# Theta behind the prediction, GpSimd's small operations ahead of the entry's low part, the last two sums in one reduction, and preparation in another order, in a gated recurrent kernel on one NeuronCore

## The reference

```python
def step(carry, xy):
    xt, yt = xy
    st, err, gs, mem, h1, c1, h2, c2 = carry
    encoded = jnp.tanh(xt @ We + st @ Ue + be)
    new_state = jnp.tanh(jnp.einsum('bd,cds->bcs', xt, Wx) + jnp.einsum('bs,cst->bct', st, Ws) + bk)
    inp = jnp.concatenate([encoded, err[:, None]], axis=1)
    mem = jnp.concatenate([inp[:, None, :], mem[:, :-1, :]], axis=1)
    a = jax.nn.relu(mem.reshape(b, -1) @ enc_w1 + enc_b1)
    agent_in = jax.nn.relu(a @ enc_w2 + enc_b2)
    h1, c1 = _lstm_cell(agent_in, h1, c1, lstm_wih1, lstm_whh1, lstm_b1)
    h2, c2 = _lstm_cell(h1, h2, c2, lstm_wih2, lstm_whh2, lstm_b2)
    gate = jax.nn.softmax(h2 @ gate_w + gate_b, axis=1)
    theta = _clamp01(jnp.mean(jnp.abs(mem[:, :10, -1]), axis=1) * 2.5)[:, None]
    gate = gate * theta + gs * (1.0 - theta)
    st = jnp.einsum('bc,bcs->bs', gate, new_state)
    pred = _clamp01(st[:, -1])
    err = pred - yt
    return ((st, err, gate, mem, h1, c1, h2, c2), pred)
```

## Time and profile before

| what | value |
|---|---|
| time, median of 3 runs | 5336.49 us (5336.03 to 5337.18) |
| the profiled execution | 5342.21 us |
| its span, first to last instruction | 5340.3 us |
| TensorE's mean granted clock | 0.998 of full speed |

### The profile page before, as it was taken

The page is one execution under the profiler, slowest core; times in us unless marked ns, Lnnn a source line. Parts: engine busy times, 40 slices in busy tenths (PEclk is TensorE's granted clock), DMA queues, the critical chain, the costliest instruction groups (busy, mean ns, idle before and its releaser), DMA issues.

```text
span 5340.3 us, 193942 instructions
## 1 busy us (share of the span) xinstructions
PE 5165.0 (97%) x68608; PEld 3158.5 (59%) x68608; DVE 4468.2 (84%) x11824; ACT 4233.4 (79%) x10241; POOL 3060.8 (57%) x6149
## 2 busy tenths in 40 slices
PE   7999999999999999999999999999999999999998
PEld 4555555555555555555555555555555555555554
DVE  7888888888888888888888888888888888888887
ACT  6887877878888878788787788788877878777886
POOL 4555555555555555555555555555555555555555
PEclk9999999999999999999999999999999999999999
DMA  2111111111111111111111111111111111111111
GB/s 68 31 30 33 30 33 30 33 30 33 30 33 30 31 31 30 33 30 33 30 33 30 33 30 33 30 32 30 30 33 30 33 30 33 30 33 30 33 30 41
DMA packets 299271, 172.29 MB, mean 32 GB/s; under 512 B 156598, under 2 KB 263866, under 8 KB 298698
## 3 DMA queue, kind: packets, MB, share of 16 engines
q1 hardware_dynamic: 293560, 159.45, 11.9%
q10 hardware_dynamic: 5138, 3.53, 0.2%
HBM read 74.55 MB, written 2.10 MB: 14 GB/s over the span
## 4 chain that ended last, share of the span: by engine, by line
PE 94%; ACT 4%; issue 2%; DVE 0%; DMA 0%; POOL 0%; ACTq 0%; POOLq 0%; DVEq 0%
PE a_ps L378 27%; PE chain L417 21%; PE a_ps L389 9%; PE cand_ps L359 8%; PE cand_ps L350 6%; PE chain L327 6%; PE chain L320 4%; ACT state_t L498 4%; PE chain L293 4%; PE a_ps L400 3%; PE cand_ps L340 3%; PE chain L434 1%; PE chain L427 0%; DMA gate_bias_stage<-in_gate_b 0%; DVE enc_table L648 0%
## 5 line engine op out<-in xcount | busy, mean ns | idle before, releaser
L378 PE MATMUL a_ps<-hist,w_hist 125*64 125x512 f16 x12288 | 1816.5, 383 | 25.2 <-DMA w_hist<-enc_table 24.0
L810 DVE TENSOR_REDUCE state<-mixed 128x64 f32<-128x512 f32 x2048 | 1353.4, 682 | 34.2 <-POOL mixed L911 0.8
L911 POOL TENSOR_TENSOR mixed<-cand,gate 128x512 f32<-128x512 f32 x1024 | 1285.3, 1277 | 48.6 <-POOL gate L899 12.5
L417 PEld LDWEIGHTS chain<-cell_in,cell_w 128*64 128x64 f32 x16384 | 903.2, 136 | 488.7 <-ACT cell_in L525 248.5
L417 PE MATMUL chain<-cell_in,cell_w 128*64 128x128 f32 x16384 | 1120.5, 277 | 41.5 <-issue 1.4
L536 ACT ACTIVATE cand<-cand_ps 128x512 f32<-128x512 f32 x2048 | 1107.0, 594 | 13.3 <-issue 0.4
L378 PEld LDWEIGHTS a_ps<-hist,w_hist 125*64 125x64 f16 x12288 | 695.8, 109 | 568.8 <-issue 298.1
L933 POOL CAST x_parts<-x_sb 128x256 f16<-128x256 f32 x512 | 203.8, 398 | 953.2 <-DVE cell_in L720 938.4
L550 ACT ACTIVATE gates<-chain 128x384 f32<-128x384 f32 x1024 | 503.5, 492 | 251.2 <-PE chain L417 251.2
L705 DVE SCALAR_TENSOR_TENSOR added<-gates 128x256 f32<-128x256 f32 x1024 | 620.8, 606 | 57.2 <-ACT gates L550 3.7
L877 POOL TENSOR_TENSOR one_theta<-ones,theta 128x8 f32<-128x8 f32 x512 | 105.3, 206 | 950.0 <-DVE theta L687 950.0
(11 more groups left out here) (80 smaller groups left out, 7348.5 us busy)
## 6 DMA issues: line engine op xcount, KB each, us to landing
x_sb<-in_x_l SPq DMA_DIRECT2D x260, 256.0 KB, 2.7
hist<-entry_parts SPq DMA_DIRECT2D x2048, 25.0 KB
w_hist<-enc_table SPq DMA_DIRECT2D x258, 128.0 KB, 2.4
y_rows<-in_y_l SPq DMA_DIRECT2D x260, 8.0 KB
ys<-in_y ACTq DMA_DIRECT2D x1, 2048.0 KB, 16.7
preds_out<-preds SPq DMA_DIRECT2D x1, 2048.0 KB, 7.5
cand<-in_encoder ACTq DMA_DIRECT2D x1, 640.0 KB, 3.8
cell_w<-in_cell ACTq DMA_DIRECT2D x2, 256.0 KB, 5.3
```

The costliest lines, as they stand in the source:

```text
L378: nc.tensor.matmul(a_ps[g][ENC * half:ENC * half + ENC, :], w_hist[0:HROWS, w_slot(u), kk, wp, :], hist[0:HROWS, xp, k, at:at + 512], star ...
L417: last = nc.tensor.matmul(chain[g][rows, P * r:P * r + P], cell_w[c][:, hf, r, :], cell_in[c][:, g, hf, :], start=False, stop=True, skip_g ...
L810: V.tensor_reduce(state[:, g, hf, 2 * pair:2 * pair + 2, :], mixed[:, pair, hf, :, :, :], AX, ALU.add)\
L911: G.tensor_tensor(mixed[:, 0, :, q, :, :], cand[:, g, 0, :, q, :, :], over_s, ALU.mult)\
```

## The change

VectorE's `thetas(cur)` goes from behind `second_hidden` to between `prediction` and `cell_terms(cur, 1)`. GpSimd's `new_error` and `keep_prediction` go ahead of `kept_share` and `kept_gate`, so that of the five small operations these two come first. The two reductions `mix_sum(old, 1, 0)` and `mix_sum(old, 1, 1)` become one over 128x1024 elements, `last_sums`, with one semaphore where there were two. In the preparation the splitting of the biases goes behind `s_ready`, and TensorE's wait for their landing goes into the first phases that use them; the first history weights are issued as soon as their table is done (`s_tables`), ahead of four of the five loads of x and y; ScalarE runs one tanh on a small cleared tile before it waits for `s_ready`.

```diff
-        q_sum = [[sem(f"q_sum{hf}_{pair}") for pair in range(2)] for hf in range(HF)]
+        q_sum = [[sem(f"q_sum0_{pair}") for pair in range(2)], [sem("q_sum1")]]
...
+            load_slot(0)
+            sp.wait_ge(s_tables, 1)
             history_weights(w_slot(-1), PER_TILE)
             history_weights(0, PER_TILE + 1)
             history_weights(1, PER_TILE + 2)
+            for t in range(1, PER_TILE):
+                load_slot(t)
+            sp.wait_ge(s_parts, 1)
+            sp.dma_start(gate_bias[1:2, :], gate_bias_low[0:1, :]).then_inc(s_fix, 16)
+            sp.dma_start(cand_bias[1:P:D_IN, :], cand_bias_low[0:P:D_IN, :]).then_inc(s_fix, 16)
+            sp.wait_ge(s_ready, 1)
...
             pe.wait_ge(s_ready, 1)
-            pe.wait_ge(s_fix, 16 * 2)
...
-                for pair in range(2):
-                    pe.wait_ge(q_sum[hf][pair], n)
+                for done in q_sum[hf]:
+                    pe.wait_ge(done, n)
...
-            def candidates_bias(item):
-                g, n, u = item
+            def candidates_bias(item, extra):
+                g, n, u = item
+                if extra is None:
+                    pe.wait_ge(s_fix, 16 * 2)
...
+            act.wait_ge(s_warm, 1)
+            nc.scalar.activation(warm[:, 1, :], warm[:, 0, :], ACT.Tanh)
             act.wait_ge(s_ready, 1)
...
+            def last_sums(item):
+                g, n, u = item
+                dve.wait_ge(q_mul[1], n + GROUPS)
+                for q in range(2):
+                    dve.wait_ge(q_mulpool[q], n + GROUPS)
+                V.tensor_reduce(state[:, g, 1, :, :].rearrange("p (a l) s -> p a (l s)", a=2),
+                                mixed[:, :, 1, :, :, :].rearrange("p a l s c -> p a (l s) c"), AX, ALU.add)\
+                    .then_inc(q_sum[1][0], 1)
...
                 if old:
-                    mix_sum(old, 1, 0)
-                    mix_sum(old, 1, 1)
+                    last_sums(old)
                 if cur:
                     error_sum(cur)
                 if old:
                     prediction(old)
                 if cur:
+                    thetas(cur)
                     cell_terms(cur, 1)
...
                 if cur:
                     second_hidden(cur)
-                    thetas(cur)
                     peaks(cur)
                     below_peak(cur)
...
                 if old:
                     next_hidden(old, cur)
+                    new_error(old, extra)
+                    keep_prediction(old, extra)
                 if cur:
                     kept_share(cur)
                     kept_gate(cur)
-                if old:
-                    new_error(old, extra)
-                    keep_prediction(old, extra)
                 if new:
                     entry_low(new)
```

More of the change, by code:

```diff
@@ L77, in recurrent_kernel @@
         ones = sb("ones", [P, TILES])
+        warm = sb("warm", [P, 2, TILES])
         x_sb = sb("x_sb", [P, PER_TILE, GROUPS, COLS])
@@ L126, in recurrent_kernel @@
         s_out, s_ys, s_hist0 = sem("s_out"), sem("s_ys"), sem("s_history_zero")
+        s_tables, s_warm = sem("s_tables"), sem("s_warm")
         s_x = [sem(f"s_x_slot{u}") for u in range(PER_TILE)]
@@ L210, in _, with load_slot @@
                 load(err_ring[:, :, 0:1], error0.rearrange("(n p o) -> p n o", p=P, o=1))
-            for t in range(PER_TILE):
+            def load_slot(t):
                 sp.dma_start(x_sb[:, t, :, :].rearrange("p g b -> p (g b)"), x_l[P * t:P * t + P, :])\
@@ L215, in _ @@
                     .then_inc(s_y[t], 16)
-            sp.wait_ge(s_parts, 1)
-            sp.dma_start(gate_bias[1:2, :], gate_bias_low[0:1, :]).then_inc(s_fix, 16)
-            sp.dma_start(cand_bias[1:P:D_IN, :], cand_bias_low[0:P:D_IN, :]).then_inc(s_fix, 16)
             def history_weights(slot, start):
@@ L225, in history_weights @@
                     .then_inc(s_wh[slot], 16)
-            sp.wait_ge(s_ready, 1)
+            load_slot(0)
+            sp.wait_ge(s_tables, 1)
             history_weights(w_slot(-1), PER_TILE)
@@ L467, in phase @@
                     cell_gates(cur, 0)
-                    candidates_bias(cur)
+                    candidates_bias(cur, extra)
                     candidates_x(cur)
@@ L610, in _ @@
             V = nc.vector
+            V.memset(warm[:, 0, :], 0.0).then_inc(s_warm, 1)
             V.memset(err_ring[:, :, :], 0.5).then_inc(s_zero, 1)
@@ L622, in _ @@
                 V.memset(gates[n][:, :, 4, :], 0.0)
-            for hf in range(HF):
-                for pair in range(2):
-                    V.memset(state[:, :, hf, 2 * pair:2 * pair + 2, :], 0.0).then_inc(q_sum[hf][pair], GROUPS)
+            for pair in range(2):
+                V.memset(state[:, :, 0, 2 * pair:2 * pair + 2, :], 0.0).then_inc(q_sum[0][pair], GROUPS)
+            V.memset(state[:, :, 1, :, :], 0.0).then_inc(q_sum[1][0], GROUPS)
             V.memset(scratch[:, :, :], 0.0).then_inc(s_prep, 1)
             dve.wait_ge(s_prep, 1)
-            dve.wait_ge(s_biases, 16 * 2)
             steps = [1]
@@ L635, in link @@
                 dve.wait_ge(s_prep, steps[0])
[L637 to L642, removed]
             dve.wait_ge(s_table, 16)
@@ L649, in _ @@
                                      enc1_table[:, start:start + m, 0, :], ALU.subtract))
+            V.tensor_copy(scratch[:, 1, :], ones[:, :]).then_inc(s_tables, 1)
             dve.wait_ge(s_load, loads[0])
@@ L676, in _ @@
             V.tensor_copy(scratch[:, 1, :], ones[:, :]).then_inc(s_ready, 1)
+            dve.wait_ge(s_biases, 16 * 2)
+            link(V.tensor_copy(cand_bias[:, :], bk_stage))
+            link(V.tensor_tensor(cand_bias_low[:, :], bk_stage, cand_bias[:, :], ALU.subtract))
+            link(V.tensor_copy(gate_bias[0:1, :], gate_bias_stage[0:1, :]))
+            V.tensor_tensor(gate_bias_low[0:1, :], gate_bias_stage[0:1, :], gate_bias[0:1, :], ALU.subtract)\
+                .then_inc(s_parts, 1)
             def error_sum(item):
@@ L815, in prediction @@
                 for hf in range(HF):
-                    for pair in range(2):
-                        dve.wait_ge(q_sum[hf][pair], n + GROUPS)
+                    for done in q_sum[hf]:
+                        dve.wait_ge(done, n + GROUPS)
                 V.tensor_scalar(pred_now[:, g, :].rearrange("p (h q) -> p h q", h=HF), state[:, g, :, :, S - 1],
```

## The result

The changed kernel takes 5219.25 us, the median of four runs (5218.74 to 5219.63), against 5336.77 for the kernel before in the same comparison: a ratio of 0.978, 95% interval 0.9763 to 0.9797, 117.5 us less. I had forecast 5255, with a range of 5205 to 5340. The profiled execution took 5219.53 us, with a span of 5217.6.

The account below looks back on a forecast made before the run. GpSimd's small operations delaying `entry_low`, and through the mixing TensorE, were taken as the bound. Per phase -0.21 + 0.06 = -0.15 us, times 511 is -77, with preparation -82: 5255 us, range 5205 to 5340.

Parts of the forecast that it names:

- What bounds the kernel: GpSimd's small operations delay `entry_low`, hence the mixing, VectorE's first-cell `cell_terms`, `first_hidden` and TensorE, by about 0.21 us a phase.
- The gain of 0.21 us a phase: `entry_low` and the mixing start 0.34 to 0.39 us earlier; TensorE can use 0.21 in the mean, bounds 0.10 and 0.23.
- The collision: GpSimd's moved small operations meet VectorE's second-cell `cell_terms` and `cell_value`: loss 0.06 us a phase, bounds 0 and 0.32.
- rival C: No collision, VectorE first each time in the second cell: 0.21 to 0.25 us a phase gained, 5205 to 5224, chance 0.20.
- Rival A: GpSimd's small operations lock VectorE out of the second cell, up to 0.35 us: around 5365 us, chance 0.12.
- The point of turning: Delay of VectorE in the second cell above which the change makes the kernel slower: 0.21 + 0.04 = 0.25 us.
- My upper bound of 0.30 to 0.35: Second-cell `cell_terms` waits for three small GpSimd operations in a row, `cell_value` then for `kept_gate`: 0.30 to 0.35 us.
- The sums: The last two reductions in one: prediction ends 0.05 to 0.13 us earlier, TensorE gains 0, bounds 0 and 0.05.
- Theta's place: Theta's 0.16 us on VectorE between prediction and second-cell `cell_terms` is covered by idle time; at most 0.16 bare.
- The preparation: Ahead of the phases: earlier table cast 1.5 us, history weights 2.5, table load 1.28; together 5.3, bounds 3 and 6.
- B: Gain absorbed: the mixing's start has another condition or the lock costs as much; only preparation left, 5331 us, chance 0.12.
- D: The small tanh makes the compiler choose a table without the exponential, switching each phase: over 1000 us more, chance 0.02.

Follow-up runs that it names:

- second run: Changed kernel plus a GpSimd copy of 128x512 numbers between idle tiles, behind `new_error` in each phase: 5391.64 us, ratio 1.0094 to the kernel before.

## Why the prediction was right or wrong

*What bounds the kernel: right.* Every link was shown. Making the mixing shorter, with nothing moved, gave the gain; so did each way of getting `entry_low` started. What carried it was the 0.28 us from the mixing's end to L705's end: over 450 phases it stays between 0.27 and 0.29, before and after.

*The gain of 0.21 us a phase: right, slightly low.* By the medians it is (117.5 - 5.3) / 511 = 0.22. The 0.232 of the two profiled executions is too high by the 5.4 us of the one before, 0.01 a phase, and holds 1.2 us of the preparation. L323 to L422 fell by 0.27 in the phase shown, as forecast; in the mean of 450 phases the step fell from 0.643 to 0.441 us, by 0.20. Some 0.03 more came between L422 and the next state transposes, a stretch that I had at nothing. That TensorE's own pace caps the step was right too: both halves of the change together give no more than one.

*Two causes for one delay.* I described the two moves as one part and didn't ask what each would do alone. Either is enough, since each takes about 0.3 us from ahead of `entry_low`, and TensorE used only 0.22.

*The collision: this step was mis-sized.* I took 0.10 us less 0.04 of slack, a loss of 0.06. The changed kernel shows no loss: the way from the last sums to the logits' load is 3.364 us in the mean, as before. 0.06 x 511 = 31 us of the 36 between 5255 and 5219; the other 5 are the gain, 0.22 and not 0.21. I had rightly argued that L712 would be first. The error came after it: I let L718 wait for one of the operations that had been held. It does start behind one (9.51, while L992 runs from 9.42 to 9.62), and keeps 0.29 us here; over 450 phases it takes at most 0.02 more, and none of that reaches TensorE. So rival C, to which I gave 0.20, had the right time, 5205 to 5224, but not the right reason: it needed VectorE to come first each time, and at L718 GpSimd comes first with an operation too short to cost anything. That the result lies in C's range is in part luck.

*Rival A, the collision as a loss: not here, but the mechanism is real.* It takes a long GpSimd instruction that reads: 0.23 us a phase with 512 numbers just ahead of `cell_terms`, 0.33 just ahead of `cell_value`. From the ratios, the latter is 1.0094 / 0.978 = 1.032 of the changed kernel, 168 us. The point of turning that I gave, a delay of 0.25 us, was 0.05 too low: a delay of 0.30 came out even with the kernel before. It cost a phase 0.23, so the slack was 0.07 and not 0.04, and the gain to be lost was 0.22 and not 0.21. In the second run the delay was 0.40 in the mean and the loss 0.33, which gives the same slack. My upper bound of 0.30 to 0.35 for the small ones was not tested as it stood: one copy of 64 numbers ahead of L715 cost nothing, and whether three in a row would hold it is not shown.

*The sums: right to give 0, for another reason.* I said that the prediction's end would come 0.05 to 0.13 us earlier and that TensorE would lose this again at the logits. The end doesn't come earlier (1.62 us behind the start of the last sums before and after), as it stands 0.02 to 0.03 us behind the end of GpSimd's copy (`next_hidden`) in each phase. The Trainium skill, "SBUF — State Buffer", section "Who interferes with whom", says that `tensor_scalar` can enter a mode that takes both ports and so excludes any GpSimd instruction, while one with two SBUF inputs excludes only those that read. The runs with the memset agree on both points: 0.73 us for a prediction of 8 numbers, and 0.29 for L721 beside the same memset. GpSimd's copy seems to hold the prediction in the same way: with the sums in one it starts 0.06 us sooner and takes 0.26 and not 0.20 us, to the same end. No run moved that copy, so this is not shown.

*Theta's place: right.* It ran in VectorE's idle time; L712 of the second cell starts as soon as the gates are there.

*The preparation: right.* Forecast 5.3 us. The first matmul came 4.0 earlier, and from the first transpose to the first L330 it went from 2.34 to 1.10, together 5.3; the run alone measured 4.6. The Trainium skill, "ScalarE: Activation LUTs", section "What ACT_TABLE_LOAD costs", gives its 2.66 us for a switch to another set, with the drain. This first load did not cost that much: without it the first state copy came 1.24 us sooner behind the first transpose, about the load's own 1.28.

*Rivals B and D* did not occur: the mixing starts as soon as the gate is there, and there is one table load.

## What to carry to other kernels

When an instruction takes twice its bare time, look for the engine that shares its port, and for a constant distance between the two ends; then go back to what starts the other engine, which can be an operation of no importance, placed just ahead of one that matters. Cap every gain by the next limit before adding up edits, since two edits that remove the same delay bring it only once. When operations are moved next to work on the shared port, what counts is who starts first, how long the first one is, and, for a VectorE instruction with two SBUF inputs, whether GpSimd's reads.

## What the runs showed of the hardware

VectorE's instruction with two SBUF inputs (256 numbers, 0.42 us by itself) ends 0.27 to 0.29 us behind the end of a GpSimd instruction that reads and started first, where its own end would come sooner than that. For 128 numbers (L721, 0.29 us by itself, beside the late copy) the distance is 0.15 us. So it isn't begun again from the start; only its last part is still to do. In the run with the small copy, a GpSimd operation of 0.26 us that started 0.19 earlier cost the 256 numbers nothing, and in the changed kernel an 8-number copy of 0.20 us cost the 128 numbers of L718 at most 0.02. A write-only memset of 0.53 us leaves such an instruction alone and holds up a `tensor_scalar` of 8 numbers; in the preparation a memset of 6.92 us holds up a cast (L647) until 0.68 us behind its end. The `tensor_scalar` had started 0.17 us ahead of the memset, when GpSimd was still at a copy: with the copy and the memset back to back, VectorE didn't get in between. In the run with the added copy at the same place it did, since the prediction (mean 0.265 us) ended 0.02 to 0.03 us behind the first copy's end. Why the two cases differ stays open.
